# A graph layer with masked attention: the first block's mask in six growing pieces, one cast held back, parts of the set-up reordered

## What is computed

```python
norm2 = jnp.linalg.norm(x, axis=1, keepdims=True)
cos = beta[0] * (x @ x.T) / (norm2 @ norm2.T + 1e-07)
masked = cos + (1.0 - adj) * -1000000000.0
x = _layernorm(x + jax.nn.softmax(masked, axis=1) @ x)
return _layernorm(x + adj @ (x @ weight))
```

## Time and profile before

| | |
|---|---|
| median of three runs | 485.62 us |
| the profiled execution | 489.12 us, of which 487.3 us are the span of its engines |
| PE busy | 471.2 us (97% of the span) |
| DVE busy | 382.3 us (78%) |
| ACT busy | 319.4 us (66%) |
| DMA queue q0 (casts) | 16.78 MB written, 41.8% of the 16 engines' span |
| DMA queue q1 (transpositions and plain loads and stores) | 29.63 MB, 31.4% |
| chain that ended last, by engine | PE 84%, DMA 12% |

### The profile page before, as it was taken

One profiled execution on the slowest core, in us unless ns is written; L12 is line 12 of the kernel. 1 busy time (PEld: TensorE's weight loads), 2 busy tenths in 40 slices (PEclk: granted clock), 3 DMA queues, 4 the chain that ended last, 5 costly groups with the idle time before them and its releaser, 6 DMA issues.

```text
span 487.3 us, 8974 instructions
## 1 busy us (share of the span) xinstructions
PE 471.2 (97%) x3551; PEld 309.3 (63%) x3551; DVE 382.3 (78%) x600; ACT 319.4 (66%) x375; POOL 58.3 (12%) x74
## 2 busy tenths in 40 slices
PE   7799969999999999999999999999999999999995
PEld 7466646676766766767677667667665444444484
DVE  4899779999999999999999999999984043222363
ACT  5899758898898889889888998988873000000000
POOL 5711011111021020102102011100100000000011
PEclk9989989999999999999999999999999999999998
DMA  8999999999999959987996999870042100111102
GB/s 197 104 120 116 89 121 134 93 130 144 128 119 140 117 84 117 142 119 67 141 113 109 112 140 138 72 144 22 0 154 67 41 23 22 44 43 44 43 24 65
DMA packets 100970, 46.78 MB, mean 96 GB/s; under 512 B 69328, under 2 KB 98384, under 8 KB 100944
## 3 DMA queue, kind: packets, MB, share of 16 engines
q0 software_dynamic: 19536, 16.78, 41.8%
q1 hardware_dynamic: 81120, 29.63, 31.4%
q10 hardware_dynamic: 288, 0.07, 0.1%
HBM read 73.99 MB, written 22.81 MB: 199 GB/s over the span
## 4 chain that ended last, share of the span: by engine, by line
PE 84%; DMA 12%; POOL 1%; issue 1%; DVE 1%; POOLq 0%; SPq 0%; DVEq 0%
PE psum L1054 22%; PE psum L995 21%; PE psum L999 11%; PE psum L972 10%; PE psum L974 10%; PE psum L973 10%; DMA adjT<-adj_bytes 6%; DMA adj_bytes<-in_adj 4%; DMA adjT<-in_x 1%; POOL rn L387 1%; DMA uT<-x_parts 1%; PE psum L1070 1%; PE psum L1071 0%; DVE E L707 0%; DVE el L715 0%
## 5 line engine op out<-in xcount | busy, mean ns | idle before, releaser
L995 PE MATMUL psum<-xaug,eh 128*128 128x257 f16 x1024 | 185.7, 275 | 3.9 <-DVE el L715 3.9
L469 ACT ACTIVATE E<-psum,sc 128x1024 f32<-128x1024 f32 x128 | 154.3, 1205 | 38.1 <-PE psum L974 37.1
L999 PE MATMUL psum<-xaug,el 128*128 128x129 f16 x1024 | 176.8, 222 | 0.0
L707 DVE SCALAR_TENSOR_TENSOR E<-E,adjT 128x1024 f32<-128x1024 f32 x128 | 156.3, 1221 | 15.4 <-ACT E L469 10.1
L715 DVE SCALAR_TENSOR_TENSOR el<-E,eh 128x1024 f16<-128x1024 f32 x128 | 155.8, 1218 | 0.0
L478 ACT ACTIVATE eh<-E 128x1024 f16<-128x1024 f32 x128 | 134.5, 1050 | 7.6 <-DVE E L707 7.3
L995 PEld LDWEIGHTS psum<-xaug,eh 128*128 128x128 f16 x1024 | 99.7, 98 | 29.1 <-DVE el L715 4.4
L1054 PE MATMUL psum<-adjT,uT 128*128 128x512 fp8e4 (+1 forms) x576 | 112.3, 355 | 0.7 <-DMA uT<-x_parts 0.7
L999 PEld LDWEIGHTS psum<-xaug,el 128*128 128x128 f16 x1024 | 100.7, 98 | 14.5
L972 PE MATMUL psum<-uT 128*128 (+1 forms) x256 | 98.1, 383 | 0.9 <-DVE uT L592 0.9
L973 PE MATMUL psum<-uT 128*128 (+1 forms) x256 | 97.6, 381 | 0.0
(11 more groups left out here) (83 smaller groups left out, 184.4 us busy)
## 6 DMA issues: line engine op xcount, KB each, us to landing
adj_bytes<-in_adj POOLq DMA_DIRECT2D x28, 512.0 KB, 12.6
x_rows<-x SPq DMA_DIRECT2D x8, 256.0 KB, 2.7
E<-x_rows SPq DMA_DIRECT2D x8, 256.0 KB, 2.9
out<-E SPq DMA_DIRECT2D x16, 128.0 KB, 2.2
adj_bytes<-in_adj POOLq DMA_DIRECT2D x7, 256.0 KB, 7.1
x_parts<-x1p SPq DMA_DIRECT2D x7, 256.0 KB, 7.3
adjT<-in_x SPq DMA_DIRECT2D x3, 512.0 KB, 6.7
uT<-x_parts SPq DMA_DIRECT2D x2, 512.0 KB, 5.6
```

The lines of the kernel that those rows point to most:

```text
L469: nc.scalar.activation(E[:, m % RING, :, :], S[m % 2], ACT.Exp, bias=col(C_BB), scale=col(C_BS)).then_inc(e_done, 1)
L707: nc.vector.scalar_tensor_tensor(out=e, in0=e, scalar=EPRE, in1=mask_bytes(b, m), op0=ALU.mult, op1=ALU.min).then_inc(masked, 1)
L995: return nc.tensor.matmul(O[t][:, 0:XC], eh[:, s, a, cols], xaug[:, j, :], start=start, stop=stop)
L999: return nc.tensor.matmul(O[t][:, 0:D + 1], el[:, s, a, cols], xaug[:, j, 0:D + 1], start=False, stop=False)
```

## The change

`FIRST` now has six pieces: one pair, one pair, two pairs, and three of four pairs, so that the last three have the size of a quarter of the later blocks. `cast_first` is as before, so C4 waits for T1 and C5 for T2. K0 waits for T3 now. K1 waits for T4 and, newly, for K0 itself to have landed. In the set-up, ACT writes the 16-bit part of group 1 ahead of its wait for the scales instead of after the first exponential, and DVE forms the rests of groups 1 and 2 ahead of the first mask. Groups 5 to 7 are written by ACT one pair later, and PE turns group 7 one pair later.

```diff
-    FIRST = [(0, 1), (1, 1), (2, 2), (4, 2), (6, 2), (8, 2), (10, 2), (12, 2), (14, 2)]
+    FIRST = [(0, 1), (1, 1), (2, 2), (4, 4), (8, 4), (12, 4)]
...
                 if k < MP + 2:
                     pool.wait_ge(first_in[len(FIRST) - 3 + k - MP], 16)
+                    if k == MP + 1:
+
+                        pool.wait_ge(piece_cast[0], 16)
                 else:
...
             uT_hi_part(0)
             unit_rows_a(1)
+            uT_hi_part(1)
             act.wait_ge(beta_ready, 2)
...
                 exp_pair(0, m)
                 if m == 0:
-                    uT_hi_part(1)
                     uT_hi_part(2)
                 if m == 1:
                     uT_hi_part(3)
                     uT_hi_part(4)
+                if m == 2:
+                    uT_hi_part(5)
+                    uT_hi_part(6)
+                    uT_hi_part(7)
                 if m in XAUG_AT:
                     xaug_hi(XAUG_AT.index(m))
                 if m > 0:
                     split_hi(0, m - 1)
-                if m == 1:
-                    uT_hi_part(5)
-                    uT_hi_part(6)
-                    uT_hi_part(7)
...
             scale_step(4)
+            uT_lo_part(1)
             small = dve.value_load(flag[0:1, 0:1], min_val=0, max_val=1)
...
                     if not tiny and m == 0:
-                        uT_lo_part(1)
+                        uT_lo_part(2)
                     mask_pair(0, m)
                     if tiny and m == 0:
-                        uT_lo_part(1)
-                    if m == 0:
                         uT_lo_part(2)
...
-                    if m == 1:
+                    if m == (2 if tiny else 1):
                         uT_lo_part(5)
                         uT_lo_part(6)
                         uT_lo_part(7)
...
                 if m == 2:
                     turn_unit_rows(5)
                     turn_unit_rows(6)
+                if m == 3:
                     turn_unit_rows(7)
```

## The result

The changed kernel is slower: 496.65 us in the median of 4 executions, against 487.28 us for the old one beside it (4 executions). The ratio is 1.021, with a 95% interval from 1.0153 to 1.0267, so the loss is clear of the noise. The forecast was 490.5 us, within 481.0 to 493.0. The direction and the place were right, the size was not. The times of the old kernel spread widely from execution to execution, and part of what follows is about that spread.

A forecast was written before the change was run, and what follows sets the result against it. PE, 97% busy, was taken as the bound, so DMAs matter only where it waits. Pair 13 weighed at 71.3 against 66.4 gave +4.9 us, added to the 485.6 us median: 490.5 us, range 481.0 to 493.0 for 8 in 10.

The forecast's parts named there:

- T2 meets T8's fate: Block 0: transposition T2, beside wide cast C3 with C4 queued, takes 17.5 us like T8 before, landing at 35.7; chance 0.48.
- A: Rival, block 0: T2 slips through at 26.8 and the old stall is gone; 3.8 us faster, 481.8 us; chance 0.28.
- B: Rival, block 0: T2 trickles only while C4 has packets, landing at 31.3; 0.5 us slower, 486.1 us; chance 0.12.
- C: Rival, block 0: T2 slips through but T3 meets C4 and C5; 7.2 us slower, 492.8 us; chance 0.12.
- The point that was to decide: Cast queues, block 0: how long before the running cast lands the next is issued; harmless at 4.25 us, holding at 6.5.
- Pair 2 and pair 1: Block 0: mask of pair 2 starts at 35.7, not 26.45; PE weighs pair 1 at 38.1, not 30.5.
- From pair 1 to pair 13: PE, block 0: 12 steps of 2.64 us from 38.1 to 69.8, plus 1.5 for the slow clock, giving 71.3.
- T4 against pair 8: Block 0: T4 lands about 52 at the latest, pair 8 is due at 51.7; a tie, counted as nothing.
- The reference point: Final sum: 4.9 us added to the old median 485.6, the profiled 489.12 us lying 3.5 above the median, giving 490.5.
- What T8's stall was worth: Old kernel ahead of pair 14: 2.7 us of PE's waiting plus 1.5 for the slow clock, 4.2 us to win.
- K1's second wait costs nothing: End of block 0: K1 delayed some 5 us, but needed at pair 20, more than 50 us after K0's issue; free.
- The rule on the cost of a DMA: Casts: a fixed 2.0 us per DMA plus bytes at 436 GB/s; each merging would save about 2 us, favouring the faster rival.

The follow-up runs named there:

- the kernel without any stall: The changed kernel with the old list of nine pieces, keeping K1's second wait and the new set-up order: 485.74 us, 1.0014 times the old kernel.

## Why the prediction was wrong, point by point

**T2 meets T8's fate: right in the outcome, not in the reason.** Called at 17.5 us, measured 19.5, and 18.9 in the chain of the kernel with the pieces alone. Holding C4 brought it to 9.4. The rivals A, B and C fell with it. The reason given was that the transposition gets no gap. The queues of the changed kernel from 24 to 28 us (packets, MB, share) say otherwise:

```profile
q1 hardware_dynamic: 600, 0.15, 126.4%
q0 software_dynamic: 42, 0.03, 9.2%
```

In those 4 us the casts moved 42 packets, where K0 had moved 406, although C4 had been issued at 21.64. The transpositions moved 600, and T2 still landed only at 37.15. So most of T2 seems to have passed in a gap, and something else held its end until C4 was nearly through (38.60). What that is stays open. The point that was to decide, between 4.25 and 6.5 us of queueing ahead, is gone too: T3 without K1 was held at 3.2.

**Pair 2 and pair 1: right in kind, 2.2 us short.** Pair 2 was called at 35.7 and came at 37.25. Between mask and rest DVE has the 0.7 us piece of xaug, which my 2.4 us left out, and T2 itself landed 1.5 us later than called. Pair 1 was weighed at 40.32, not 38.1.

**From pair 1 to pair 13: 0.8 us short.** Called 31.7 + 1.5 = 33.2, measured 74.32 - 40.32 = 34.0. The 1.5 us for the slow clock had been read after a gap of 3.9 us. After one of 9.5 us, PE worked at half clock for over 5 us and lost 2.5 in the first step alone. T4 against pair 8, counted as a tie, was none: DVE waited 2.62 us. At PE only about 0.6 of that arrived (its steps from pair 6 to pair 9 are 2.81, 2.64 and 3.09 us), since PE trailed DVE there. That does not make T4 harmless: it is the link of the chain, and had T2 alone been cured and T4 landed when it did, pair 9 would have been weighed at 64.8 all the same. My 2.64 per step was also 1.4 us too much over the block in both kernels, because pairs 11 and 12 are weighed without scores between them (a kernel without the stall has pair 1 at 30.15 and pair 13 at 60.48, 30.3 and not 31.7). The slow clock hid that. These terms make 2.2 + 0.8 = 3.0 us, and profiled against profiled the change cost 497.01 - 489.12 = 7.9 where I had 4.9. That closes the sum between the profiled executions.

**The reference point: this step failed, and it is half of the miss.** "Against that median, which the result is compared with, it is 485.6 + 4.9": I took the difference between two profiled executions and added it to a median, as if both kernels' profiled executions lay 3.5 us above their medians. The old one's did, against the three runs known then. The new one's lies 0.4 above (497.01 against 496.65). That is 3.1 us, the 3.0 us above are the rest, and together they are the 6.1 us from 490.5 to 496.65. The likely reason for the unequal distance is that the old profiled execution held T8's stall and many of the others do not, while the changed kernel's executions all lie close together. I had noted the 3.5 us without asking what they held. So the credit for removing T8's stall was there in some executions only: without K1 the median falls by 1.1 us. Against an execution free of the stall the price is 13.5 us on PE's line, and the medians moved by 9.4 (by the ratio, 10.2).

**What T8's stall was worth: 5.6 us, not 4.2.** The pace of 62.2 for pair 13 was the same 1.4 us too late as above. With K1 held, the first pair of block 1 was weighed at 69.68 instead of 75.48, 5.8 us earlier, and the span of the kernel without any stall is 5.6 us shorter. The sum of the forecast takes the old side as measured, so this figure does not enter it. In rival A the same 1.4 us made the gain too small.

**K1's second wait costs nothing: wrong by a little, and it did nothing in the changed kernel.** In the old kernel it removes T8's stall in the profile and puts 1.73 us ahead of pair 20. Pair 20 was not "more than 50 us" away from K0's issue: in the old kernel its mask came at 78.55, 38 us after it. In the changed kernel the wait ends nothing: K0 landed at 53.73, and K1 was issued at 56.83, when T4 had landed (56.55). Pair 14 is free there without it, as the kernel with the pieces alone shows. All pairs come later, and U1 is in time. Casts and set-up were otherwise worth nothing, as called.

**The rule on the cost of a DMA.** The fixed cost per DMA in "DMA: Bandwidth & Descriptors" of the Trainium skill ("Anatomy of one DMA") spoke for wide pieces. A wide cast alone took 9.7 to 10.5 us here, a narrow one 6.5 beside another. From issue to landing the wide ones are cheaper per byte, as that rule has it. In a queue this did not show: in the old kernel the narrow casts C3 to C8 landed every 4.5 us, 9.1 for four pairs, the wide ones, each issued some 0.5 us after the one before had landed, every 10.3. And what was waited for was not the cast but the transposition beside it. The same page of the Trainium skill, in "Queues, rings and completion order", has each DMA engine take turns between queues, packet by packet. The near one-to-one count at 52:56 in the earlier trace rows agrees with it. It does not explain a transposition that is held while the casts move next to nothing.

## What to carry to other kernels

Where small transfers on one queue must get past large ones on another, ask of each small one which large transfer runs when it is issued and whether the next is queued before that one ends. Where it is, allow for the small one landing only with the second. Here merging the large ones turned this from an accident of some executions into the rule, and holding one back cured the transposition concerned at the price of the held one's own deadline. And before pricing a stall from a profile, ask whether the profiled execution is a typical one: if it lies above the median by about the stall's price, the stall may not be in the median at all. Compare medians with medians and profiled executions with profiled ones.

## What the hardware showed that I had not expected

- A transposition of two pairs took 12.4 us beside one wide cast with a narrow one behind, 12.5 between narrow casts queued two deep, 14.3 to 19.5 with two wide ones, and 7.3 to 9.5 beside one wide cast with nothing behind. Between narrow casts at the old depth T3 took 4.7 to 8.2 us in eight profiles and 11.3 in one.
- The same kernel seems to meet the stall in some executions and not in others (483.0 to 490.0 us, inferred from times), while with C3 and C4 both wide it was there in both profiles, and all executions lay between 495.1 and 497.6.
- The same eight instructions of POOL ahead of C4 took 3.76 us in the old kernel's trace and 5.36 in the changed one's:

```profile
16.33 5.36 POOL L396 TENSOR_SCALAR adjT<-adjT,rn 128x128 f32<-128x128 f32 x8
21.64 0.67 POOL L386 DMA_DIRECT2D adj_bytes<-in_adj  x1
```

- With them, C4 was issued 1.55 us later than in the earlier trace rows, and T2 was held nonetheless. What slows these instructions was not looked into.
